# Expert dispatch with one coded product per unit, and routing scans that read PSUM

## The chip, the cores and the metric

The kernel runs on one core of a Trainium2 chip. The metric is the device time in microseconds (us) of one execution; of several executions the median is taken. A core has the engines TensorE (PE in the profile; its weight loads are PEld), VectorE (DVE), ScalarE (ACT), GpSimd (POOL) and SyncE (SP), which run their own instruction streams and wait for each other on semaphores.

## The reference, cut to what matters

One decoder layer: self-attention, cross-attention, then a block of attention and a mixture of experts, on 64 x 256 = 16384 tokens of 256 features. The change touches the part between the router's logits and the experts. Each token picks two of 8 experts; its place in an expert's list is the number of earlier tokens that picked that expert, first choices counted before second choices; an expert takes 4096 tokens.

```python
        logits = x @ wr                                   # x: 16384 tokens x 256, wr: 256 x 8
        top1 = jnp.argmax(probs, axis=-1)
        m1 = jax.nn.one_hot(top1, N_EXPERTS, dtype=x.dtype)
        top2 = jnp.argmax(jnp.where(m1 > 0, -jnp.inf, logits), axis=-1)
        m2 = jax.nn.one_hot(top2, N_EXPERTS, dtype=x.dtype)
        loc1 = jnp.cumsum(m1, axis=0) - 1.0
        loc2 = jnp.cumsum(m2, axis=0) - 1.0 + m1.sum(0, keepdims=True)
        ...
        buf = buf.at[top1, s1].set(x, mode='drop')
        buf = buf.at[top2, s2].set(x, mode='drop')
        h = jax.nn.relu(jnp.einsum('ecd,edf->ecf', buf, w1) + b1[:, None, :])
        y = (jnp.einsum('ecf,efd->ecd', h, w2) + b2[:, None, :]) * (1.0 - MOE_TOKEN_DROPOUT)
        ...
        return g1[:, None] * y1 + g2[:, None] * y2
```

## The kernel before

`program` builds six stages one after the other, with a barrier of all engines between them: `prepare`, three `attention` stages (A, X, F), then `route`, `dispatch` and `experts`. The change is in `route` and `dispatch`.

**Layout.** Token number n*128 + p stands in partition p at tile n, so the logits are a tile of 128 partitions x 128 tiles x 8 experts (`[P, NT, NE]`, 1024 values a partition).

**`route`.** VectorE does nearly all of it in one chain in which each instruction waits for the one before (`chain.step`). It copies the logits to `first`, finds the maximum over experts (`top`), marks it, takes the lowest expert among equals (`rank`), and writes the one-hot choice `one` in float32 and a copy `one_b` in bf16 (L1238, L1239). This happens twice, for the first and the second choice. TensorE multiplies each `one_b` by a matrix of ones below the diagonal (`inside`: earlier tokens of the same tile) and by one of all ones (`whole`: tokens of a tile for each expert), both in PSUM. VectorE then copies `whole` to `hit` (L1250), runs one running sum over tiles for each of 8 experts (L1252), subtracts `hit` again to get the sum of the earlier tiles only (L1254), adds `inside` (L1255), for the second choice also adds the totals of the first (L1258), and picks the token's own expert (L1259, L1260). From that come `scatter`, the place in the list of 8 x 4096 places, split into `high` (which 128-block of the list, 0 to 255) and `low` (which place in the block), and `tail`, the gates.

**`dispatch`.** It inverts that map: for each of the 32768 places, which token stands there. The result is `token` (`[P, 256]`, place low in the partition, block high in the column). There are U = 256 units, one for each tile and choice. For a unit, VectorE writes two tiles of "lines": `by_row` (128 tokens x 128 places: 1 + token's row at the place `low`, else 0, L1335) and `block_of` (128 tokens x 256 blocks: 1 at the block `high`, else 0, L1337). ScalarE scales `by_row` by (1 + tile)/(1 + row) to give `by_tile` (L1352). TensorE multiplies `by_row` by `block_of` into `row_sum` (L1360) and `by_tile` by `block_of` into `tile_sum` (L1362), and both sums run over all 256 units in PSUM. The tiles of lines have R = 4 buffers: VectorE waits on `summed` before it writes one again. At the end four VectorE instructions turn the two sums into `token` (L1340 to L1343). SyncE sends `tail` to the token rows in DRAM at the stage's start (L1311).

**`experts`.** GpSimd gathers token rows by `token` (L1547), TensorE does the two matrix products of each expert (L1466, L1476), ScalarE and VectorE read them out, GpSimd adds the gated rows to the output. Its first instructions come after the barrier behind `dispatch`.

Program order alone sets the order of the work here; the loops over units are written out in full.

Of the kernel before, what the change touches and what calls it, by code (L numbers as in the profile page):

```python
# [5 lines left out]
ALU = mybir.AluOpType  # L6
ACT = mybir.ActivationFunctionType
AX = mybir.AxisListType
P = 128
# [1143 lines left out]
NE = 8  # L1153
# [3 lines left out]
def route(nc, C, D, io):  # L1157
# [3 lines left out]
    with ExitStack() as ctx:  # L1161
# [3 lines left out]
        one = [sb(f"one{i}", [P, NT, NE]) for i in range(2)]  # L1165
        one_b = [sb(f"one_b{i}", [P, NT, NE], BF16) for i in range(2)]
        loc = sb("loc", [P, NT, NE])
        run = [sb(f"run{i}", [P, NT, NE]) for i in range(2)]
# [13 lines left out]
        link, hot, counted, spread_in, exped, b1_in, b1_turned = (  # L1182
            sem(n) for n in ("link", "hot", "counted", "spread_in", "exped", "b1_in", "b1_turned"))
# [7 lines left out]
        def halves(t):  # L1191
            return flat(t).rearrange("p (a w) -> p a w", a=HALF) if HALF > 1 else flat(t)

# [3 lines left out]
        with nc.Block() as block:  # L1197
# [5 lines left out]
            def _(pe):  # L1203
                for i in range(2):
                    pe.wait_ge(hot, i + 1)
                    for a in range(HALF):
                        m = flat(one_b[i])[:, a * W:(a + 1) * W]
# [15 lines left out]
            def _(dve):  # L1223
# [6 lines left out]
                chain.step(v.tensor_copy(flat(first), flat(L)))  # L1230
                down3 = down[:, :].unsqueeze(1).broadcast_to([P, NT, NE])
                for i in range(2):

                    chain.step(v.tensor_reduce(top[i][:, :], first[:, :, :], AX.X, ALU.max))
                    chain.step(v.tensor_tensor(hit[:, :, :], first[:, :, :], wide(top[i]), ALU.is_equal))
# [3 lines left out]
                    v.tensor_copy(flat(one_b[i]), flat(one[i])).then_inc(hot, 1)  # L1239
                    if i == 0:  # L1240
                        chain.step(v.scalar_tensor_tensor(flat(first), flat(one[0]), -3e38, flat(first), ALU.mult, ALU.add))
# [436 lines left out]
```

## Time and profile before

| | us |
|---|---|
| median of 3 executions (5968.39 to 5971.0) | 5969.68 |
| the profiled execution's own time | 5964.57 |
| its span, first to last instruction | 5962.9 |
| `route`, first to last VectorE instruction | 3932.60 to 3984.04 |
| `dispatch`, first to last VectorE instruction | 3985.02 to 4096.76 |
| `experts`, from its first VectorE instruction | 4097.99 |

Times in rows are us from the span's start. A row of the timeline gives start, duration, engine, line, operation and tiles; its duration is that of one instruction from start to end, and neighbours on an engine can overlap, so the step from one start to the next is what a stream costs. Means of one instruction are in ns.

### The profile page before, as it was taken

The page shows a single profiled execution, that of the slowest core. Times are in us where ns is not written, and L with a number is a line of the kernel's source. Part 1 is how long each engine was busy: PE and PEld are TensorE (multiplying, and loading weights), DVE is VectorE, ACT ScalarE, POOL GpSimd, SP SyncE. Part 2 cuts the span into 40 slices and gives each one's busy share as a digit, 9 for nine tenths or more (in the row PEclk, how much of TensorE's full clock was granted, in tenths as well). Part 3 has the DMA queues.
Part 4 walks back from the last instruction along what each step waited for, and adds up shares of the span by engine and source line. Part 5 has one row for each costly group of instructions (what it writes and reads, how often), then busy time and mean ns, then how long its engine had stood idle before and what let it go on. Part 6 is the DMA issues. An engine that isn't in the chain of part 4 may idle for free. (4 is left out here: it accounts for less than half of the span.)

```text
span 5962.9 us, 144169 instructions
## 1 busy us (share of the span) xinstructions
PE 5621.1 (94%) x44441; PEld 4031.8 (68%) x44441; DVE 3721.2 (62%) x10169; ACT 3120.9 (52%) x6803; POOL 2036.6 (34%) x1753
## 2 busy tenths in 40 slices
PE   0999999989999999799999999958999999999998
PEld 0677777667777777577777777734666666666666
DVE  7888888778888887688888888875111111111111
ACT  4788888746666666477777777635121111211111
POOL 0322222233333333244444444401333333333332
PEclk9999999989999999999999999979999999999999
DMA  5777777556666665466766666631222222222221
GB/s 157 178 184 182 182 185 180 148 159 175 174 173 173 174 174 166 120 178 170 182 171 175 177 170 181 168 26 49 39 53 51 33 49 53 32 45 51 38 39 20
DMA packets 625511, 750.10 MB, mean 126 GB/s; under 512 B 131075, under 2 KB 554188, under 8 KB 625328
## 3 DMA queue, kind: packets, MB, share of 16 engines
q1 hardware_dynamic: 568992, 679.62, 43.7%
q0 software_dynamic: 49152, 63.10, 6.6%
q10 hardware_dynamic: 7184, 5.00, 0.3%
q8 instruction: 108, 1.77, 0.1%
q14 instruction: 75, 0.61, 0.0%
HBM read 476.49 MB, written 272.24 MB: 126 GB/s over the span
## 5 line engine op out<-in xcount | busy, mean ns | idle before, releaser
L1488 ACT ACTIVATE exp_hT<-exp_hid,exp_b 128x512 f32<-128x512 f32 x512 | 351.8, 687 | 1487.3 <-PE exp_hid L1466 1372.3
L1476 PE MATMUL exp_res<-exp_w,exp_hT 128*128 128x256 f32 x4096 | 901.2, 381 | 0.8 <-ACT exp_hT L1488 0.8
L1466 PE MATMUL exp_hid<-exp_xT,exp_w 128*128 128x512 f32 x2048 | 891.0, 593 | 0.9 <-DVE exp_xT L1496 0.9
L1476 PEld LDWEIGHTS exp_res<-exp_w,exp_hT 128*128 128x128 f32 x4096 | 773.8, 190 | 112.2 <-ACT exp_hT L1488 1.6
L1566 POOL DMA_INDIRECT out_dram<-exp_gated,exp_token x256 | 406.1, 1586 | 1099.4 <-issue 412.7
L931 DVE TENSOR_REDUCE F_tops<-F_score 128x2 f32<-128x512 f32 x1024 | 684.3, 686 | 59.8 <-PE F_score L685 40.8
L822 ACT ACTIVATE F_probs<-F_scoreT 128x512 f32<-128x512 f32 x1024 | 583.8, 590 | 236.8 <-PE F_scoreT L654 236.8
L1466 PEld LDWEIGHTS exp_hid<-exp_xT,exp_w 128*128 128x128 f32 x2048 | 389.8, 191 | 464.6 <-issue 458.5
L1496 DVE COPY exp_xT<-exp_turn 128x512 f32<-128x512 f32 x128 | 82.6, 686 | 803.2 <-PE exp_turn L1450 803.2
L931 DVE TENSOR_REDUCE A_tops<-A_score 128x3 f32<-128x384 f32 x1024 | 531.6, 554 | 62.3 <-PE A_score L671 54.0
L1532 DVE SCALAR_TENSOR_TENSOR exp_y<-exp_res,exp_b2s 128x512 f32<-128x512 f32 x128 | 88.5, 692 | 735.4 <-PE exp_res L1476 735.4
L822 ACT ACTIVATE A_probs<-A_scoreT 128x384 f32<-128x384 f32 x1024 | 451.0, 488 | 23.1 <-PE A_scoreT L642 14.7
L654 PE MATMUL F_scoreT<-QS,KS 98*128 98x256 bf16 x2048 | 365.4, 275 | 9.7 <-ACT F_probs L822 1.5
L685 PE MATMUL F_score<-KS,QS 96*128 96x256 bf16 x2048 | 362.7, 274 | 8.3 <-DMA KS<-d_k 7.4
L931 DVE TENSOR_REDUCE X_tops<-X_score 128x4 f32<-128x484 f32 x512 | 329.8, 658 | 29.0 <-PE X_score L680 28.9
L822 ACT ACTIVATE X_probs<-X_scoreT 121x512 f32<-121x512 f32 x512 | 295.1, 595 | 78.3 <-PE X_scoreT L650 72.6
L1547 POOL DMA_INDIRECT exp_x<-d_h,exp_token x256 | 269.1, 1051 | 195.6 <-DMA exp_w<-in_L_ffn_w_dram 117.9
L666 PE MATMUL A_score<-causal,ident_b 128*128 128x256 bf16 x1024 | 282.8, 276 | 12.1 <-DMA KS<-d_k 8.3
L638 PE MATMUL A_scoreT<-ident_b,causal 128*128 128x128 bf16 x2048 | 286.1, 221 | 3.2 <-ACT A_probs L822 1.1
L669 PE MATMUL A_score<-KS,QS 96*128 96x256 bf16 x1024 | 281.2, 275 | 0.0
L711 PE MATMUL F_outs<-F_probs,V 128*32 128x256 f32 x4096 | 275.4, 387 | 1.9 <-ACT F_outT L831 1.9
L642 PE MATMUL A_scoreT<-QS,KS 98*128 98x256 bf16 x1024 | 277.2, 271 | 0.0
(330 smaller groups left out, 12099.1 us busy)
## 6 DMA issues: line engine op xcount, KB each, us to landing
QS<-d_q SPq DMA_DIRECT2D x384, 192.0 KB, 3.6
KS<-d_k SPq DMA_DIRECT2D x256, 192.0 KB, 4.0
QS<-d_q SPq DMA_DIRECT2D x384, 128.0 KB, 3.9
KS<-d_k SPq DMA_DIRECT2D x256, 128.0 KB, 4.0
d_q<-A_q_parts SPq DMA_DIRECT2D x64, 384.0 KB, 3.6
d_k<-A_k_parts SPq DMA_DIRECT2D x64, 384.0 KB, 3.9
QS<-d_q SPq DMA_DIRECT2D x384, 64.0 KB, 3.7
d_q<-X_q_parts SPq DMA_DIRECT2D x64, 384.0 KB, 4.0
```

What stands on the lines that cost most here:

```text
L638: mm(s[:, n * P:(n + 1) * P], C["causal"][:, 0:P], ident_b[:, :], start=n == 0, stop=False, skip_group_check=True)
L642: last = mm(s[:, P:384], k[0:98, i, 0:P], q[0:98, i, :], start=False, stop=True, skip_group_check=True)
L654: last = mm(s[:, n * 256:(n + 1) * 256], k[0:98, i, n * P:(n + 1) * P], q[0:98, i, :], start=True, stop=True)
L666: mm(s[:, 0:384].rearrange("p (n k) -> p n k", n=3)[:, 0:3:2, :], ident_b[:, :], C["causal"][:, :].rearrange("p (n k) -> p n k", n=2), sta ...
L669: mm(s[:, P:384], q[0:96, i, P:256], k[0:96, i, :], start=False, stop=False, skip_group_check=True)
L685: last = mm(s[:, n * 256:(n + 1) * 256], q[0:96, i, n * P:(n + 1) * P], k[0:96, i, :], start=True, stop=True)
L822: nc.scalar.activation(probs[m % 2][0:KR, at:at + HB, :].rearrange("p u x -> p (u x)"), scoreT[i % TB][0:KR, 0:HB * TCOL], ACT.Exp)\
L931: nc.vector.tensor_reduce(dst, src, AX.X, ALU.max).then_inc(score_read, 1)
L1466: last = nc.tensor.matmul(h[:, :], w1[k][:, a, f * P:(f + 1) * P], xT[par][:, a, :], start=a == 0, stop=a == 1)
L1476: last = nc.tensor.matmul(res[t][:, s, :], hT[par][:, f, (2 * t + s) * P:(2 * t + s + 1) * P], w2[k][:, f, :], start=f == 0, stop=f == NF - 1)
L1488: nc.scalar.activation(hT[par][:, f, :], hid[f % 2][:, :], ACT.Relu, bias=b1[k][:, f:f + 1])\
L1566: nc.gpsimd.indirect_dma_start(out, bass.IndirectOffsetOnAxis(token[j % (2 * XB)][:, s:s + 1], 0), gated[par][:, s, :], None, bounds_check ...
```

## The change

**In `route`:** `one` is bf16 and is the matrix product's operand, so the casts to `one_b` are gone and TensorE waits on the chain's own semaphore. The first maximum reads the logits in place, so the copy to `first` is gone. The 8 running sums read `whole` straight from PSUM, with a step of 8 values, and write `run` one tile further on (`run` has 129 tiles, its tile 0 is zero or, for the second choice, the first choice's totals, which are also each sum's starting value, given by a pointer). `run[0:128]` is then the sum of the earlier tiles by itself; the copy to `hit`, the subtraction and the addition of totals are gone.

**In `dispatch`:** one product per unit. `by_row` holds 1 + row/128 at the place, `block_of` holds 2^(tile - 64) at the block. Their product is a float whose exponent is the tile and whose upper mantissa bits are the row; the upper 16 bits of the sum, less a constant, are the token's number. `by_tile` and `tile_sum` are gone. Of every five units VectorE writes the lines of four (205 of 256, ring of R = 6) and ScalarE those of the fifth (51 units, ring of RA = 2), in two steps: |column - low| and |column - high| (`gaps`, Abs with a pointer bias), then Relu(value - value * gap), which is the value where the gap is 0 and 0 elsewhere. The gaps of the next ScalarE unit are issued ahead of the second step of this one. TensorE takes the units in their old order.

```diff
--- before.py
+++ after.py
@@ -1162,10 +1162,9 @@
-        one = [sb(f"one{i}", [P, NT, NE]) for i in range(2)]
-        one_b = [sb(f"one_b{i}", [P, NT, NE], BF16) for i in range(2)]
+        one = [sb(f"one{i}", [P, NT, NE], BF16) for i in range(2)]
         loc = sb("loc", [P, NT, NE])
-        run = [sb(f"run{i}", [P, NT, NE]) for i in range(2)]
+        run = [sb(f"run{i}", [P, NT + 1, NE]) for i in range(2)]
...
+        def by_expert(t):
+            return t[:, :, :].rearrange("p a (n e) -> p (a n) e", e=NE)
+
+        def earlier_tiles(i):
+            return run[i][:, 0:NT, :].rearrange("p n e -> p (n e)").rearrange("p (a w) -> p a w", a=HALF)
...
-                    pe.wait_ge(hot, i + 1)
+                    pe.wait_ge(link, CHOSEN[i])
                     for a in range(HALF):
-                        m = flat(one_b[i])[:, a * W:(a + 1) * W]
+                        m = flat(one[i])[:, a * W:(a + 1) * W]
...
-                chain.step(v.tensor_copy(flat(first), flat(L)))
+                v.memset(run[0][:, 0, :], 0.0)
                 down3 = down[:, :].unsqueeze(1).broadcast_to([P, NT, NE])
                 for i in range(2):
-                    chain.step(v.tensor_reduce(top[i][:, :], first[:, :, :], AX.X, ALU.max))
-                    chain.step(v.tensor_tensor(hit[:, :, :], first[:, :, :], wide(top[i]), ALU.is_equal))
+                    scores = (L, first)[i]
+                    chain.step(v.tensor_reduce(top[i][:, :], scores[:, :, :], AX.X, ALU.max))
+                    chain.step(v.tensor_tensor(hit[:, :, :], scores[:, :, :], wide(top[i]), ALU.is_equal))
                     chain.step(v.tensor_tensor(hit[:, :, :], hit[:, :, :], down3, ALU.mult))
                     chain.step(v.tensor_reduce(rank[i][:, :], hit[:, :, :], AX.X, ALU.max))
                     chain.step(v.tensor_tensor(one[i][:, :, :], wide(rank[i]), down3, ALU.is_equal))
-                    v.tensor_copy(flat(one_b[i]), flat(one[i])).then_inc(hot, 1)
+                    assert chain.done == CHOSEN[i]
                     if i == 0:
-                        chain.step(v.scalar_tensor_tensor(flat(first), flat(one[0]), -3e38, flat(first), ALU.mult, ALU.add))
+                        chain.step(v.scalar_tensor_tensor(flat(first), flat(one[0]), -3e38, flat(L), ALU.mult, ALU.add))
...
-                    chain.step(v.tensor_copy(halves(hit), cols(whole[i])))
+                    if i == 1:
+                        chain.step(v.tensor_copy(run[1][:, 0, :], run[0][:, NT, :]))
                     for e in range(NE):
-                        last = v.tensor_tensor_scan(run[i][:, :, e], ones[:, :], hit[:, :, e], 0.0, ALU.mult, ALU.add)
+                        before = 0.0 if i == 0 else run[0][:, NT, e:e + 1]
+                        last = v.tensor_tensor_scan(run[i][:, 1:NT + 1, e], ones[:, :], by_expert(whole[i])[:, :, e], before,
+                                                    ALU.mult, ALU.add)
                     chain.step(last)
-                    chain.step(v.tensor_tensor(flat(loc), flat(run[i]), flat(hit), ALU.subtract))
-                    chain.step(v.tensor_tensor(halves(loc), cols(inside[i]), halves(loc), ALU.add))
-                    if i == 1:
-                        every = run[0][:, NT - 1:NT, :].broadcast_to([P, NT, NE])
-                        chain.step(v.tensor_tensor(loc[:, :, :], loc[:, :, :], every, ALU.add))
+                    chain.step(v.tensor_tensor(halves(loc), cols(inside[i]), earlier_tiles(i), ALU.add))
...
-    R = 4
+    R, RA = 6, 2
     U = 2 * NT
+    SHARE = 5
+    BIAS = 127 - NT // 2
...
+        ON_ACT = [u for u in range(U) if u % SHARE == SHARE - 1]
+        ON_DVE = [u for u in range(U) if u % SHARE != SHARE - 1]
+        powers = power[:, :].bitcast(F32)
...
-                chain = Chain(dve, link, 0, 10, C["passed"])
...
+                chain = Chain(dve, link, 0, 16, C["passed"])
+                chain.step(v.tensor_scalar(place[:, :], C["number"][:, :], 7, None, ALU.logical_shift_right))
+                chain.step(v.tensor_scalar(place[:, :], place[:, :], BIAS, None, ALU.add))
+                chain.step(v.tensor_scalar(power[:, :], place[:, :], 23, None, ALU.logical_shift_left))
+                chain.step(v.tensor_copy(row1[:, :], C["number"][:, 0:1]))
+                chain.step(v.tensor_scalar(row1[:, :], row1[:, :], 1.0 / P, 1.0, ALU.mult, ALU.add))
+                chain.step(v.tensor_scalar(minus[:, :], row1[:, :], -1.0, None, ALU.mult))
+                for i in range(2):
+                    chain.step(v.tensor_scalar(low_minus[i][:, :], C["low"][i][:, :], -1.0, None, ALU.mult))
+                    chain.step(v.tensor_scalar(high_minus[i][:, :], C["high"][i][:, :], -1.0, None, ALU.mult))
                 dve.wait_ge(numbered, 1)
                 chain.step(v.tensor_copy(columns[:, :], column[:, :]))
-                for u in range(U):
-                    n, i, k = u // 2, u % 2, u % R
-                    need(dve, summed, u - R + 1)
+                for d, u in enumerate(ON_DVE):
+                    n, i, k = u // 2, u % 2, d % R
+                    if d >= R:
+                        dve.wait_ge(summed, ON_DVE[d - R] + 1)
                     v.tensor_scalar(by_row[k][:, :], columns[:, 0:P], C["low"][i][:, n:n + 1], row1[:, :],
+                                    ALU.is_equal, ALU.mult)
+                    v.tensor_scalar(block_of[k][:, :], columns[:, :], C["high"][i][:, n:n + 1], powers[:, n:n + 1],
                                     ALU.is_equal, ALU.mult).then_inc(built, 1)
-                    v.tensor_scalar(block_of[k][:, :], columns[:, :], C["high"][i][:, n:n + 1], None, ALU.is_equal)\
-                        .then_inc(built, 1)
                 dve.wait_ge(summed, U)
-                chain.step(v.tensor_copy(rows_of[:, :], row_sum[:, :]))
-                chain.step(v.scalar_tensor_tensor(number[:, :], tile_sum[:, :], float(P), rows_of[:, :], ALU.mult, ALU.add))
+                chain.step(v.tensor_copy(codes[:, :], code_sum[:, :]))
+                chain.step(v.tensor_scalar(upper[:, :], codes[:, :].bitcast(I32), 16, None, ALU.logical_shift_right))
+                chain.step(v.tensor_copy(number[:, :], upper[:, :]))
                 chain.step(v.tensor_scalar(nothing[:, :], number[:, :], 0.0, float(2 ** 20), ALU.is_equal, ALU.mult))
-                v.scalar_tensor_tensor(C["token"][:, :], number[:, :], -float(P + 1), nothing[:, :], ALU.add, ALU.add)\
-                    .then_inc(link, 1)
-                dve.wait_ge(link, 11)
+                chain.step(v.scalar_tensor_tensor(C["token"][:, :], number[:, :], -float(P * BIAS), nothing[:, :], ALU.add,
+                                                  ALU.add))
+                chain.close()
 
             @block.scalar
             def _(act):
-                for u in range(U):
-                    n, k = u // 2, u % R
-                    act.wait_ge(built, 2 * u + 1)
-                    nc.scalar.activation(by_tile[k][:, :], by_row[k][:, :], ACT.Copy, scale=ratio[:, n:n + 1])\
-                        .then_inc(scaled, 1)
+                def gaps(a):
+                    n, i, k = ON_ACT[a] // 2, ON_ACT[a] % 2, a % RA
+                    need(act, shaped, a - RA + 1)
+                    nc.scalar.activation(row_gap[k][:, :], columns[:, 0:P], ACT.Abs, bias=low_minus[i][:, n:n + 1])
+                    nc.scalar.activation(block_gap[k][:, :], columns[:, :], ACT.Abs, bias=high_minus[i][:, n:n + 1])\
+                        .then_inc(spaced, 1)
+
+                act.wait_ge(link, 11)
+                gaps(0)
+                for a, u in enumerate(ON_ACT):
+                    n, k = u // 2, a % RA
+                    if a + 1 < len(ON_ACT):
+                        gaps(a + 1)
+                    act.wait_ge(spaced, a + 1)
+                    if a >= RA:
+                        act.wait_ge(summed, ON_ACT[a - RA] + 1)
+                    nc.scalar.activation(row_a[k][:, :], row_gap[k][:, :], ACT.Relu, bias=row1[:, :], scale=minus[:, :])
+                    nc.scalar.activation(block_a[k][:, :], block_gap[k][:, :], ACT.Relu, bias=powers[:, n:n + 1],
+                                         scale=-(2.0 ** (n - NT // 2))).then_inc(shaped, 1)
 
             @block.tensor
             def _(pe):
                 for u in range(U):
-                    k = u % R
-                    pe.wait_ge(built, 2 * u + 2)
-                    nc.tensor.matmul(row_sum[:, :], by_row[k][:, :], block_of[k][:, :], start=u == 0, stop=u == U - 1)
-                    pe.wait_ge(scaled, u + 1)
-                    nc.tensor.matmul(tile_sum[:, :], by_tile[k][:, :], block_of[k][:, :], start=u == 0, stop=u == U - 1)\
-                        .then_inc(summed, 1)
+                    if u in ON_ACT:
+                        a = ON_ACT.index(u)
+                        pe.wait_ge(shaped, a + 1)
+                        row, blocks = row_a[a % RA], block_a[a % RA]
+                    else:
+                        d = ON_DVE.index(u)
+                        pe.wait_ge(built, d + 1)
+                        row, blocks = by_row[d % R], block_of[d % R]
+                    nc.tensor.matmul(code_sum[:, :], row[:, :], blocks[:, :], start=u == 0, stop=u == U - 1).then_inc(summed, 1)
```

What stands on VectorE between the products and the places of the second choice in `route`, before (`whole` and `inside` are the products in PSUM, `run` the running sums, `one` the choice):

```order
L1250 COPY route_hit<-route_whole 128x1024
L1252 SCALAR_TENSOR_TENSOR route_run<-route_ones,route_hit 128x128 x8
L1254 TENSOR_TENSOR route_loc<-route_run,route_hit 128x1024
L1255 TENSOR_TENSOR route_loc<-route_inside,route_loc 128x1024
L1258 TENSOR_TENSOR route_loc<-route_loc,route_run 128x1024
L1259 TENSOR_TENSOR route_loc<-route_loc,route_one 128x1024
```

and now:

```order
L1258 COPY route_run<-route_run 128x8
L1261 SCALAR_TENSOR_TENSOR route_run<-route_ones,route_run,route_whole 128x128 x8
L1264 TENSOR_TENSOR route_loc<-route_inside,route_run 128x1024
L1265 TENSOR_TENSOR route_loc<-route_loc,route_one 128x1024
```

Two 1024-value instructions around the eight sums (L1250, L1254) and the addition of totals (L1258) are gone, and a copy of 8 values has come (L1258 of the changed kernel). The sums now have a third operand, the starting value. The first choice reads the same without L1258 on either side.

VectorE from the start of `dispatch` to its first unit, before (each later unit repeats the last two rows):

```order
L1324 CAST disp_place<-number 128x128
L1325 TENSOR_SCALAR disp_row<-disp_place 128x1
L1326 TENSOR_SCALAR disp_tile<-disp_place 128x128
L1327 TENSOR_SCALAR disp_tile<-disp_tile 128x128
L1328 RECIPROCAL disp_ratio<-disp_row 128x1
L1329 TENSOR_SCALAR disp_ratio<-disp_tile,disp_ratio 128x128
L1331 CAST disp_columns<-disp_column 128x256
L1335 TENSOR_SCALAR disp_by_row<-disp_columns,low,disp_row 128x128
L1337 TENSOR_SCALAR disp_block_of<-disp_columns,high 128x256
```

and now, behind a first shift (L1339):

```order
L1340 TENSOR_SCALAR disp_place<-disp_place 128x128
L1341 TENSOR_SCALAR disp_power<-disp_place 128x128
L1342 CAST disp_row<-number 128x1
L1343 TENSOR_SCALAR disp_row<-disp_row 128x1
L1344 TENSOR_SCALAR disp_minus<-disp_row 128x1
L1346 TENSOR_SCALAR disp_low_minus<-low 128x128
L1347 TENSOR_SCALAR disp_high_minus<-high 128x128
L1346 TENSOR_SCALAR disp_low_minus<-low 128x128
L1347 TENSOR_SCALAR disp_high_minus<-high 128x128
L1349 CAST disp_columns<-disp_column 128x256
L1354 TENSOR_SCALAR disp_by_row<-disp_columns,low,disp_row 128x128
L1356 TENSOR_SCALAR disp_block_of<-disp_columns,high,disp_power 128x256
```

There are four more instructions ahead of the first unit, and `block_of` reads a second pointer (`power`). The pair of the last two rows stands 205 times instead of 256.

ScalarE from `route` to the end of the unit loop, before:

```order
L1219 ACTIVATE route_other<-route_spread 128x1024
L1220 ACTIVATE route_prob<-route_total 128x128
L1197 UNCONDITIONAL_BRANCH
L1347 UNCONDITIONAL_BRANCH
L1352 ACTIVATE disp_by_tile<-disp_by_row,disp_ratio 128x128 x256
```

and at the start of the loop now (`row_gap` and `block_gap` are the distances, `row_a` and `block_a` the lines):

```order
L1372 ACTIVATE disp_row_gap<-disp_columns,disp_low_minus 128x128
L1373 ACTIVATE disp_block_gap<-disp_columns,disp_high_minus 128x256
L1372 ACTIVATE disp_row_gap<-disp_columns,disp_low_minus 128x128
L1373 ACTIVATE disp_block_gap<-disp_columns,disp_high_minus 128x256
L1385 ACTIVATE disp_row_a<-disp_row_gap,disp_row,disp_minus 128x128
L1386 ACTIVATE disp_block_a<-disp_block_gap,disp_power 128x256
L1372 ACTIVATE disp_row_gap<-disp_columns,disp_low_minus 128x128
L1373 ACTIVATE disp_block_gap<-disp_columns,disp_high_minus 128x256
L1385 ACTIVATE disp_row_a<-disp_row_gap,disp_row,disp_minus 128x128
L1386 ACTIVATE disp_block_a<-disp_block_gap,disp_power 128x256
```

One instruction per unit has become four for every fifth unit, two of 128 and two of 256 columns; a pair of gaps runs one ScalarE unit ahead.

## Rows read from the trace of the kernel before

**Rows 1.** The page: busy us (share of span) xinstructions, and TensorE's granted clock in 40 slices.
```profile
PE 5621.1 (94%) x44441; PEld 4031.8 (68%) x44441; DVE 3721.2 (62%) x10169; ACT 3120.9 (52%) x6803; POOL 2036.6 (34%) x1753
...
PEclk9999999989999999999999999979999999999999
```

**Rows 2.** Busy time by window: PE, PEld, DVE, ACT, POOL; clock; DMA share; GB/s.
```profile
4000.00:4050.00 50.00, 50.00 (x240) 22.83 (x239) 50.00 (x240) 47.88 (x120) 0.00 (x0) 1.00 0.22 2
...
4095.00:4113.00 18.00, 0.05 (x1) 0.00 (x0) 5.42 (x11) 0.00 (x0) 7.61 (x8) 0.60 0.79 264
4113.00:4120.00 7.00, 5.79 (x14) 3.40 (x15) 2.00 (x7) 0.31 (x1) 4.72 (x5) 0.56 0.59 178
```

**Rows 3.** Groups by form, 3984.5 to 4098: busy us, mean ns | idle before, releaser.
```profile
L1352 ACT ACTIVATE disp_by_tile<-disp_by_row,disp_ratio 128x128 bf16<-128x128 bf16 x256 | 102.8, 401 | 40.4 <-DVE disp_by_row L1335 35.8
L1335 DVE TENSOR_SCALAR disp_by_row<-disp_columns,low,disp_row 128x128 bf16<-128x128 bf16 x256 | 76.2, 298 | 0.0
L1360 PE MATMUL disp_row_sum<-disp_block_of,disp_by_row 128*128 128x256 bf16 x256 | 74.1, 289 | 3.9 <-DVE disp_block_of L1337 3.9
...
L1337 DVE TENSOR_SCALAR disp_block_of<-disp_columns,high 128x256 bf16<-128x256 bf16 x256 | 69.0, 269 | 0.0
```

**Rows 4.** Timeline at the start of `dispatch` and of its unit loop.
```profile
3985.02 0.41 DVE L1324 CAST disp_place<-number 128x128 f32<-128x128 int32 x1 [0.97 <-PEq L84]
...
3987.08 0.32 DVE L1335 TENSOR_SCALAR disp_by_row<-disp_columns,low,disp_row 128x128 bf16<-128x128 bf16 x1
3987.31 0.28 DVE L1337 TENSOR_SCALAR disp_block_of<-disp_columns,high 128x256 bf16<-128x256 bf16 x1
...
3987.50 0.31 DVE L1335 TENSOR_SCALAR disp_by_row<-disp_columns,low,disp_row 128x128 bf16<-128x128 bf16 x1
...
3988.07 0.42 PE L1360 MATMUL disp_row_sum<-disp_block_of,disp_by_row 128*128 128x256 bf16 x1
```

**Rows 5.** Timeline at the end of the unit loop.
```profile
4094.20 0.27 DVE L1337 TENSOR_SCALAR disp_block_of<-disp_columns,high 128x256 bf16<-128x256 bf16 x1
...
4095.09 0.43 DVE L1340 COPY disp_rows_of<-disp_row_sum 128x256 f32<-128x256 f32 x1 [0.62 <-PE disp_tile_sum L1362]
4095.55 0.42 DVE L1341 SCALAR_TENSOR_TENSOR disp_number<-disp_tile_sum,disp_rows_of 128x256 f32<-128x256 f32 x1
4096.01 0.29 DVE L1342 TENSOR_SCALAR disp_nothing<-disp_number 128x256 f32<-128x256 f32 x1
```

**Rows 6.** Timeline of `route`, the VectorE instructions that the change touches.
```profile
3933.17 0.63 DVE L1230 COPY route_first<-logits 128x1024 f32<-128x1024 f32 x1
...
3940.12 0.69 DVE L1239 CAST route_one_b<-route_one 128x1024 bf16<-128x1024 f32 x1
3940.73 1.22 DVE L1241 SCALAR_TENSOR_TENSOR route_first<-route_one,route_first 128x1024 f32<-128x1024 f32 x1
...
3954.18 1.22 DVE L1250 COPY route_hit<-route_whole 128x1024 f32<-128x1024 f32 x1
3955.44 2.64 DVE L1252 TENSOR_TENSOR_SCAN route_run<-route_ones,route_hit 128x128 f32<-128x128 f32 x8
3958.11 1.23 DVE L1254 TENSOR_TENSOR route_loc<-route_run,route_hit 128x1024 f32<-128x1024 f32 x1
3959.37 1.23 DVE L1255 TENSOR_TENSOR route_loc<-route_inside,route_loc 128x1024 f32<-128x1024 f32 x1
```

**Rows 7.** Groups by form, VectorE, whole span: same operation with zero, one, two pointers.
```profile
L1018 DVE TENSOR_SCALAR F_xw<-F_xin,F_mean_var,F_rstd 128x256 f32<-128x256 f32 x128 | 51.9, 406 | 0.0
...
L1516 DVE TENSOR_SCALAR exp_b2s<-exp_b 128x256 f32<-128x256 f32 x16 | 4.0, 292 | 0.0
...
L1329 DVE TENSOR_SCALAR disp_ratio<-disp_tile,disp_ratio 128x128 f32<-128x128 f32 x1 | 0.3, 286 | 0.0
...
L1327 DVE TENSOR_SCALAR disp_tile<-disp_tile 128x128 f32<-128x128 f32 x1 | 0.2, 226 | 0.0
```

**Rows 8.** Timeline of ScalarE in `route`: two instructions without pointers.
```profile
3950.33 1.06 ACT L1219 ACTIVATE route_other<-route_spread 128x1024 f32<-128x1024 f32 x1 [20.93 <-DVE route_total L1243]
3951.29 0.29 ACT L1220 ACTIVATE route_prob<-route_total 128x128 f32<-128x128 f32 x1
```

**Rows 9.** DMA issues, 3980 to 4100: KB, us to landing.
```profile
d_h<-tail SPq DMA_DIRECT2D x1, 192.0 KB, 24.7
```

More of the change, by code:

```diff
@@ L1181, in route @@
         whole = [ps(f"whole{i}", [P, HALF, 512]) for i in range(2)]
-        link, hot, counted, spread_in, exped, b1_in, b1_turned = (
-            sem(n) for n in ("link", "hot", "counted", "spread_in", "exped", "b1_in", "b1_turned"))
+        CHOSEN = (5, 11)
+        assert W == 512
+        link, counted, spread_in, exped, b1_in, b1_turned = (
+            sem(n) for n in ("link", "counted", "spread_in", "exped", "b1_in", "b1_turned"))
         def flat(t):
@@ L1299, in dispatch @@
         column, columns = sb("column", [P, HI], I32), sb("columns", [P, HI], BF16)
-        place, row1, tile1, ratio = sb("place", [P, NT]), sb("row1", [P, 1]), sb("tile1", [P, NT]), sb("ratio", [P, NT])
-        by_row, by_tile = [[sb(f"{n}{k}", [P, P], BF16) for k in range(R)] for n in ("by_row", "by_tile")]
-        block_of = [sb(f"block_of{k}", [P, HI], BF16) for k in range(R)]
-        rows_of, number, nothing = sb("rows_of", [P, HI]), sb("number", [P, HI]), sb("nothing", [P, HI])
-        row_sum, tile_sum = ps("row_sum", [P, HI]), ps("tile_sum", [P, HI])
-        numbered, link, built, scaled, summed, tail_out = (
-            sem(n) for n in ("numbered", "link", "built", "scaled", "summed", "tail_out"))
+        place, power = sb("place", [P, NT], I32), sb("power", [P, NT], I32)
+        row1, minus = sb("row1", [P, 1]), sb("minus", [P, 1])
+        low_minus, high_minus = [[sb(f"{n}{i}", [P, NT]) for i in range(2)] for n in ("low_minus", "high_minus")]
+        by_row, block_of = ([sb(f"{n}{k}", [P, m], BF16) for k in range(R)] for n, m in (("by_row", P), ("block_of", HI)))
+        row_gap, block_gap = ([sb(f"{n}{k}", [P, m]) for k in range(RA)] for n, m in (("row_gap", P), ("block_gap", HI)))
+        row_a, block_a = ([sb(f"{n}{k}", [P, m], BF16) for k in range(RA)] for n, m in (("row_a", P), ("block_a", HI)))
+        codes, number, nothing = sb("codes", [P, HI]), sb("number", [P, HI]), sb("nothing", [P, HI])
+        upper = sb("upper", [P, HI], I32)
+        code_sum = ps("code_sum", [P, HI])
+        numbered, link, built, spaced, shaped, summed, tail_out = (
+            sem(n) for n in ("numbered", "link", "built", "spaced", "shaped", "summed", "tail_out"))
+        ON_ACT = [u for u in range(U) if u % SHARE == SHARE - 1]
+        ON_DVE = [u for u in range(U) if u % SHARE != SHARE - 1]
+        powers = power[:, :].bitcast(F32)
         with nc.Block() as block:
@@ L1322, in _ @@
                 v = nc.vector
-                chain = Chain(dve, link, 0, 10, C["passed"])
-                chain.step(v.tensor_copy(place[:, :], C["number"][:, :]))
-                chain.step(v.tensor_scalar(row1[:, :], place[:, 0:1], 1.0, None, ALU.add))
-                chain.step(v.tensor_scalar(tile1[:, :], place[:, :], place[:, 0:1], 1.0 / P, ALU.subtract, ALU.mult))
-                chain.step(v.tensor_scalar(tile1[:, :], tile1[:, :], 1.0, None, ALU.add))
-                chain.step(v.reciprocal(ratio[:, 0:1], row1[:, :]))
@@ L1329, in _ @@
-                chain.step(v.tensor_scalar(ratio[:, :], tile1[:, :], ratio[:, 0:1], None, ALU.mult))
+                chain = Chain(dve, link, 0, 16, C["passed"])
[3 more added lines that the diff above has]
+                chain.step(v.tensor_copy(row1[:, :], C["number"][:, 0:1]))
```

## The prediction

> **What bounds the kernel now.** I read the page's engine line first, then the busy time by window over `dispatch`, the groups by form, the timeline at the loop's two ends, and the timeline of `route`. Over the span TensorE is the busy engine, 94% [rows 1], but that says nothing of the two stages that change. In `route` TensorE has eight products and one transpose; VectorE works through one chain in which each instruction waits for the one before, so each instruction removed gives its whole step back. In the unit loop of `dispatch` four columns are to be compared: VectorE is busy for 50.00 of 50 us, ScalarE for 47.88, TensorE for 50.00 [rows 2]. Three engines look full; one is. A TensorE product is 0.28 to 0.42 us from start to end but they overlap, so its row says little. ScalarE's instruction takes 0.401 [rows 3] against a unit's 0.419, and where ScalarE does not wait it starts the next instruction 0.10 before the last has ended (3950.33 + 1.06 against 3951.29 [rows 8]), so it could go at about 0.30. VectorE has no idle time [rows 3], and it goes at its steady pace from the first unit, when no buffer has yet been used twice: 3987.08, 3987.31, 3987.50, steps of 0.23 and 0.19 [rows 4]. So VectorE sets the pace: (4094.20 - 3987.08 - 0.23) / 255 = 0.419 us a unit [rows 4, 5], 107.3 us for 256. `experts` starts behind a barrier, so what the two stages lose, the span loses.
>
> **`route`, step by step.** Steps are start to start. The copy to `first`: 0.66 (0.63 and 0.03 of hand-over). Two casts: 3940.12 to 3940.73, 0.61 each, 1.22. Two copies of `whole`: 3954.18 to 3955.44, 1.26 each, 2.52. Two subtractions: 3958.11 to 3959.37, 1.26 each, 2.52. One addition of totals, the same form and size: 1.25. Removed: 8.17 [rows 6]. Added: a memset of 8 values, 0.03 (hidden in its neighbours' overlap), and a copy of 8 values, 0.2 (below the 0.226 of a 128-column instruction [rows 7]). Eight of the sixteen running sums get a pointer as starting value. A pointer costs (406 - 292)/2 = 57 ns in the same operation and size with two pointers and with none, and 286 - 226 = 60 ns with one [rows 7]; I take 8 x 0.057 = 0.46, between 0 and 0.9 (twice the row). The sums also read PSUM in place of SBUF. Nothing in the trace shows a running sum from PSUM. The nearest rows are L1255, which reads PSUM, and L1254, which does not: 1.23 both [rows 6]; I take 0. The other end: a plain copy goes from 0.63 (SBUF) to 1.22 (PSUM), so an operand in PSUM can cost a fast rate; the sums take 2.64/8 = 0.33 a step, and if they lost 0.13 each it would be 2.1. A gain is excluded: the same values are read. `one` in bf16 changes nothing for instructions with a second operand that run at 1.22 now. TensorE's products start 0.6 earlier and were long done when read. Sum: -8.17 + 0.03 + 0.2 + 0.46 = -7.5 us.
>
> By the Trainium skill ("VectorE: DVE Perf Modes", section "The TRN2 errata") a VectorE instruction has a fixed part of 58 cycles from SBUF and 120 from PSUM, at 0.96 GHz 65 ns more for each sum; by that rule 16 sums would cost 1.0 us more and the total would be 1.0 us less gain. The trace does not agree for 1024 values, 1.22 to 1.23 us from either memory [rows 6].
>
> **`dispatch`, ahead of the loop.** Now 3985.02 to 3987.08, 2.06 [rows 4]. Then: the first, 0.44; two more shifts of 128 columns at 0.226 + 0.03 = 0.26 [rows 7]; three of one column at about 0.19; four sign changes of 128 columns at 0.26; the cast of `columns`, 0.33: 2.9. Cost +0.8.
>
> **The loop.** `by_row` stays in form. `block_of` gets a second pointer: 0.269 becomes 0.326, the unit 0.419 + 0.057 = 0.476. VectorE has 205 units: 205 x 0.476 = 97.6 against 107.3, -9.7 us. The second pointer is the one price that matters. Below: 0, if it is read beside the first; then 205 x 0.419 = 85.9, -21.4. Above: 0.11, what a pointer costs ScalarE (0.401 with one [rows 3] against 0.29 [rows 8]); then 108.4, +1.1. I take 0.057 because the form with two pointers is there in both element sizes: `by_row` and `block_of` differ by 0.298 - 0.269 = 0.029 with half the columns, which fits 0.057 for the pointer less 0.028 for 128 columns [rows 3, 7].
>
> What is late next? ScalarE: per unit of its own two instructions of 128 and two of 256 columns. From 0.29 for 128 and 1.06 for 1024 a column costs 0.86 ns [rows 8], so 256 take 0.40; a pointer adds 0.11. `row_gap` 0.40, `block_gap` 0.51, `row_a` (two pointers) 0.51, `block_a` 0.51: 1.93 end to end, 1.63 with three overlaps of 0.10, about 1.66 with the wait on its own `shaped`. It has 4 x 0.476 = 1.90 for that. Behind its wait on `summed` (two ScalarE units back, ten units) only its own lines are queued, and TensorE waits for those; VectorE could go ten units before it would notice. At the start ScalarE needs about 2.4 us to its first unit against VectorE's 1.9, which the ring of six covers. TensorE has one product a unit; in the first units, where a product still takes 0.42 from start to end [rows 4], two of them fit into each unit of 0.419, so one fits into 0.476 whatever the clock.
>
> **Behind the loop.** From the last `block_of` to the first read of the sums it is 0.89 now, with ScalarE's copy in between; then 0.33 + 0.28 to 0.42 + 0.06, about 0.15 less. Four closing instructions of 1.67 become five: 0.46 + 3 x 0.33 + 0.42 = 1.87, +0.2 [rows 5]. Together +0.05. SyncE's store of `tail` lands in 24.7 us [rows 9], well inside 98. TensorE's granted clock is 0.60 over the 18 us behind `dispatch` and 0.56 in the next 7 [rows 2], so `experts` starts at the lower level already; at worst 0.50 for 0.56, 0.4 us.
>
> **Sum.** -7.5 + 0.8 - 9.7 + 0.05 = -16.3 us. The profiled execution of 5964.57 becomes 5948.3 us; the median shown is 5.1 above it, so 5969.68 becomes 5953.4.
>
> **Rivals.**
> *The pointer is cheaper than its row* or VectorE's pairs close up further: between -20 and -28 in all, so 5942 to 5950. For it: durations overlap by 0.07 in the loop, and a pointer read could fall there. Against: `by_row` has two and its step, 0.23, is longer than that of `block_of`, 0.19, with twice the columns [rows 4].
> *ScalarE sets the pace.* If its instructions don't overlap (each waits somewhere) a period is 1.93 to 2.07 (four hand-overs of 0.03 more). At 2.0: 51 x 2.0 = 102.0 and 0.9 of lead for the first gaps, 102.9, -4.4 in the loop, -11.1 in all: 5958.6. For it: three of its waits in each unit. Against: all three are on events long past in steady state but the one on `shaped`, and the pairs have no wait inside.
> *`block_of` loses its fast rate* with the second pointer: the slower side. At present it goes at about 0.22 ns a column (the 0.028 above). In float32 the rate is about 0.5 ns ((292 - 226)/128 [rows 7]), in L1254 about 1.04. At that last rate it costs 256 x 0.82 = 0.21 more: 0.686 x 205 = 140.6, +33.3, in all +26.6, 5996.3. At the middle rate the unit is 0.553 and the total -0.6. It turns slower by over 0.2% when a unit takes more than (107.3 + 6.7 + 11.9)/205 = 0.614. Against it: `by_row` has the same form, two pointers and two operations, and 0.298 leaves no room for it.
>
> **Chances.** Forecast as worked out, 0.63, its own range 5950 to 5957. Cheaper pointer 0.17. ScalarE's pace 0.12, a third of it still over the bound. Lost rate 0.06, of which the slowest rate 0.04. Something that gives it back in `experts`, 0.02. The measurement tells about 0.2%, 11.9 us, from no change. Faster 0.63 + 0.17 + 0.04, less 0.03 for noise near the bound: 0.81. Slower 0.05. Same 0.14. The range: 5943, most of the way to the cheap pointer, to 5962, past ScalarE's pace at 2.07 (51 x 2.07 + 0.9, -7.1 in all less the noise).
>
> **What will show it.** `block_of` at about 326 ns and steps of 0.23 and 0.25 in the loop; VectorE without idle time in it and ScalarE idle for 0.2 us or so of each 1.9; the loop in 97 to 98 us; sums in `route` at 0.40 us, eight of them at 0.46. `route` should end 7.5 us earlier. I am wrong if TensorE's waits in the loop are on ScalarE, if `block_of` takes over 0.40, or if the sums from PSUM take over 0.5 each.

## The result and the profile after

| | before | after |
|---|---|---|
| median of 8 executions, us | 5969.49 (5966.25 to 5971.43) | 5952.72 (5949.35 to 5956.41) |
| span of the profiled execution, us | 5962.9 | 5951.0 |

The ratio is 0.9971, its 95% interval 0.996 to 0.9982: the changed kernel is faster by 16.8 us in the medians, by 17 us by the ratio (11 to 24). The forecast was 16.3 us less and 5953.4 us.

The spans differ by 11.9 only. The unchanged stages explain it: `route` begins at 3932.6 us in the profile of before and at 3936.5 in that of after, and in the ten other profiles of this study at 3935.4 to 3939.6. The profile of before was early by 2.8 us or more against all the others, which accounts for over half of the 5 us by which it lay under its median. So stages are compared within each profile. From the first VectorE instruction of `route` to the first of `experts` it is 4097.99 - 3932.60 = 165.4 us before and 4086.20 - 3936.50 = 149.7 after, 15.7 less. From there to the end it is 1864.9 and 1864.8 us: these two profiles show nothing given back, though the same stage takes up to 1866.0 us in other profiles of this study, and 1870.0 in one, so a few tenths would not be seen.

The interval of 11 to 24 us is too wide to test single terms of the forecast; they are tested in the stages below.

Groups by form in `dispatch` of the changed kernel (busy us, mean ns | idle before, releaser), which answer to [rows 3]:

```profile
L1356 DVE TENSOR_SCALAR disp_block_of<-disp_columns,high,disp_power 128x256 bf16<-128x256 bf16 x205 | 67.6, 330 | 0.0
L1354 DVE TENSOR_SCALAR disp_by_row<-disp_columns,low,disp_row 128x128 bf16<-128x128 bf16 x205 | 61.1, 298 | 0.0
L1386 ACT ACTIVATE disp_block_a<-disp_block_gap,disp_power 128x256 bf16<-128x256 f32 x51 | 25.1, 492 | 0.0
L1373 ACT ACTIVATE disp_block_gap<-disp_columns,disp_high_minus 128x256 f32<-128x256 bf16 x51 | 25.1, 492 | 0.0
L1385 ACT ACTIVATE disp_row_a<-disp_row_gap,disp_row,disp_minus 128x128 bf16<-128x128 f32 x51 | 25.0, 491 | 8.9 <-PE disp_code_sum L1400 8.9
```

`block_of` went from 269 to 330 ns, `by_row` stayed at 298, and VectorE still has no idle time. ScalarE's waits are on TensorE (8.9 us), which waits for VectorE's lines: it is ScalarE that has time to spare. The longest waits of the loop show it (who waited for whom: us in total, times, longest us):

```profile
PEld disp_code_sum L1400 <- DVE disp_block_of L1356: 79.7, 204, 5.0
...
PEld disp_code_sum L1400 <- ACT disp_block_a L1386: 0.2, 1, 0.2
```

The timeline at the start of the loop and at its end, for [rows 4, 5]:

```profile
3981.38 0.40 DVE L1339 TENSOR_SCALAR disp_place<-number 128x128 int32<-128x128 int32 x1 [0.98 <-PEq L84]
...
3984.28 0.32 DVE L1354 TENSOR_SCALAR disp_by_row<-disp_columns,low,disp_row 128x128 bf16<-128x128 bf16 x1
3984.51 0.34 DVE L1356 TENSOR_SCALAR disp_block_of<-disp_columns,high,disp_power 128x256 bf16<-128x256 bf16 x1
...
3984.77 0.31 DVE L1354 TENSOR_SCALAR disp_by_row<-disp_columns,low,disp_row 128x128 bf16<-128x128 bf16 x1
...
3986.59 0.40 ACT L1372 ACTIVATE disp_row_gap<-disp_columns,disp_low_minus 128x128 f32<-128x128 bf16 x1
...
3988.20 0.40 ACT L1372 ACTIVATE disp_row_gap<-disp_columns,disp_low_minus 128x128 f32<-128x128 bf16 x1
```

```profile
4082.30 0.33 DVE L1356 TENSOR_SCALAR disp_block_of<-disp_columns,high,disp_power 128x256 bf16<-128x256 bf16 x1
...
4083.11 0.42 DVE L1359 COPY disp_codes<-disp_code_sum 128x256 f32<-128x256 f32 x1 [0.49 <-PE disp_code_sum L1400]
4083.57 0.29 DVE L1360 TENSOR_SCALAR disp_upper<-disp_codes 128x256 int32<-128x256 int32 x1
...
4084.56 0.42 DVE L1363 SCALAR_TENSOR_TENSOR token<-disp_number,disp_nothing 128x256 int32<-128x256 f32 x1
```

The steps are 0.23 and 0.26 where they were 0.23 and 0.19. The loop, first `by_row` to last `block_of`, takes 98.0 us where it took 107.1. A ScalarE unit takes 3988.20 - 3986.59 = 1.61 us while ScalarE is not yet ahead and waits for nothing.

The sums and their neighbours in `route`, for [rows 6]:

```profile
3956.22 2.60 DVE L1261 TENSOR_TENSOR_SCAN route_run<-route_ones,route_whole 128x128 f32<-128x128 f32 x8
3958.85 1.23 DVE L1264 TENSOR_TENSOR route_loc<-route_inside,route_run 128x1024 f32<-128x1024 f32 x1
...
3965.96 0.17 DVE L1258 COPY route_run<-route_run 128x8 f32<-128x8 f32 x1
3966.17 3.08 DVE L1261 TENSOR_TENSOR_SCAN route_run<-route_ones,route_run,route_whole 128x128 f32<-128x128 f32 x8
```

From PSUM eight sums take 2.60 us, from SBUF they took 2.64. With a starting value by pointer they take 3.08, so (3.08 - 2.60)/8 = 0.06 us for each pointer. `route` ends 43.7 us after its first VectorE instruction started, before 51.2 (to the start of its last one).

### The profile page after: what moved, and what is told of

It reads as the page before. It is cut to its first block and busy times, and to the rows that moved or that the text cites. A ratio compares the mean times of both kernels' runs of the same rounds, so it can differ in the third digit from the quotient of the medians.

```text
span 5951.0 us, 143551 instructions
## 1 busy us (share of the span) xinstructions
PE 5601.1 (94%) x44185; PEld 4006.4 (67%) x44185; DVE 3714.2 (62%) x10066; ACT 3103.8 (52%) x6751; POOL 2037.1 (34%) x1753
```

## Experiments

In all of them "the loop" is from the start of the first `by_row` to that of the last `block_of`, and "the two stages" from the first VectorE instruction of `route` to the first of `experts`. Ratios are to the kernel before on the same chip. Where a single execution is given, only its stages are read.

### The two parts apart

Route alone (the kernel before with the new `route`):

> The kernel before with the new route alone. Theory (every step removed from VectorE's chain is given back whole): route is 7.5 us shorter from its first VectorE instruction to the last, dispatch as before at 111.7 us, 5969.5 - 7.5 = 5962.0 us. Rival (part of route's chain waits for something else, so the steps are not given back whole): the trace's route is shorter by less than 7, or dispatch gets longer by what route gained, and the time is 5965 to 5969.

Measured: 5963.43 us, ratio 0.9987 (0.9978 to 0.9996). That is 7.6 us under the kernel before on the same chip. The two stages take 157.8 us, 7.6 less (165.39 - 157.84 = 7.55); the loop is 107.0.

Dispatch alone (the kernel before with the new `dispatch`):

> The kernel before with the new dispatch alone. Theory (the unit loop's pace is VectorE's, 0.479 us for each of its 205 units): the loop takes 98.0 us in place of 107.1, the lines ahead and behind cost 1.0 more, 5969.5 - 8.2 = 5961.3 us. Rival (the two parts need each other, because places arrive earlier or the clock at the start of dispatch differs): the loop is not 98 us here. The gains of this run and of the one with route alone should add up to the 15.7 us that the two stages lost in the profile of the changed kernel.

Measured: 5965.41 us, ratio 0.999 (0.9981 to 0.9999). The two stages take 157.3 us, 8.1 less; the loop is 98.1. The median is 4 us above the expectation, of which 1.6 can be the chip (the kernel before has 5971.07 here, 5969.49 above). The profile's two stages are as expected, but its `experts` took 1870.0 us from the first VectorE instruction, against 1864.8 to 1866.0 in the other profiles, though its code is the same; why it did so in that execution was not found. In the profiles 7.55 + 8.10 = 15.65 is what the two stages lost together (15.69), so the parts add up, and neither hid behind the other. The medians alone, 7.6 and 5.7 less than the kernel before, could not show this: their intervals are 11 us wide.

### The second pointer

```diff
-  v.tensor_scalar(block_of[k][:, :], columns[:, :], C["high"][i][:, n:n + 1], powers[:, n:n + 1],
+  v.tensor_scalar(block_of[k][:, :], columns[:, :], C["high"][i][:, n:n + 1], 2.0 ** (n - NT // 2),
                   ALU.is_equal, ALU.mult)
```

> The changed kernel, with the power of two of block_of given as an immediate: it is the same in every partition, 2^(tile-64). Theory (VectorE sets the pace and the pointer costs 57 to 61 ns an instruction): block_of goes from 330 to about 272 ns, the unit from 0.479 to 0.421, the loop from 98.0 to 86.3 us, 5952.7 - 11.7 = 5941.0 us, and ScalarE, at 1.61 us a unit of its own against VectorE's 1.68 for four, is just short of setting the pace. Rival A (ScalarE or its hand-shake with TensorE sets the pace already; ScalarE waits 8.9 us on summed): the loop stays at 97 to 98 us. Rival B (any second operation costs it, pointer or not): block_of stays at 330 ns and the loop at 98.

Measured: 5941.54 us, ratio 0.9949 (0.9935 to 0.9963). It is the fastest kernel of this study (it comes once more below, as the immediate alone). By tile (min/median/max ns, first and last start):

```profile
L1354 DVE TENSOR_SCALAR disp_by_row<-disp_columns,low,disp_row x205: 302/323/355, 3986.1 to 4071.5; 128x128 bf16<-128x128 bf16 x103
L1356 DVE TENSOR_SCALAR disp_block_of<-disp_columns,high x205: 274/295/328, 3986.3 to 4071.7; 128x256 bf16<-128x256 bf16 x103
```

From the timeline's starts the loop is 4071.74 - 3986.05 = 85.7 us, 12.3 less, so the pointer cost 12.3/205 = 0.060 us a unit. Rivals A and B both fall. The duration did not come as expected, 295 ns and not 272, and `by_row`, which nobody touched, went from 297 to 323; yet the unit fell to 0.419. The price is in the steps, not in the durations.

### Who sets the pace

No unit on ScalarE:

```diff
-        ON_ACT = [u for u in range(U) if u % SHARE == SHARE - 1]
-        ON_DVE = [u for u in range(U) if u % SHARE != SHARE - 1]
+        ON_ACT = []
+        ON_DVE = list(range(U))
```

> The changed kernel, but VectorE writes the lines of all 256 units and ScalarE none. Theory (VectorE's pace): 256 x 0.479 = 122.7 us in the loop, 24.7 longer than with the share, so the coded product without the share would be 15.6 us slower in the loop than the old loop of 107.1; time about 5977. Rival (TensorE at the lower clock, or the ring, sets the pace): the loop stays near 98 us.

Measured (one execution, 5980.64 us): the first `by_row` and the last `block_of` are

```profile
3987.31 0.32 DVE L1354 TENSOR_SCALAR disp_by_row<-disp_columns,low,disp_row 128x128 bf16<-128x128 bf16 x1
...
4109.85 0.33 DVE L1356 TENSOR_SCALAR disp_block_of<-disp_columns,high,disp_power 128x256 bf16<-128x256 bf16 x1
```

The loop takes 122.5 us, so the rival falls. The coded product without the share is slower than the kernel before, because all it does for VectorE is to add a pointer.

Every fourth unit on ScalarE:

```diff
-    SHARE = 5
+    SHARE = 4
```

> The changed kernel with every fourth unit on ScalarE instead of every fifth. Theory (the slower of the two engines sets the pace: VectorE 3 x 0.479 = 1.44 us, ScalarE 1.61 us a period of four units): ScalarE becomes the bound, 64 x 1.61 = 103 us in the loop, 5 longer than with every fifth, with VectorE waiting some 10 us in all. Rival (ScalarE's share has slack left, because its 1.61 holds waits that go away): the loop follows VectorE, 192 x 0.479 = 92 us.

Measured (one execution): the loop is 101.1 us. Its longest waits (who waited for whom: us in total, times, longest us):

```profile
PEld disp_code_sum L1400 <- ACT disp_block_a L1386: 65.9, 63, 1.1
...
PE disp_code_sum L1400 <- ACT disp_block_a L1386: 36.3, 63, 0.6
```

TensorE's products wait for ScalarE in 63 periods, where in the changed kernel its weight loads wait for VectorE. ScalarE sets the pace, 63 x 1.61 = 101.4. The rival falls. At its own pace VectorE would take 192 x 0.479 = 92.0 us, so it loses 9.1 in the loop; its idle column shows 4.5 of that, since in an undisturbed stream the next instruction starts before the last has ended. The expected 103 counts all 64 ScalarE units. The last unit of all is now ScalarE's, and the first read of the sum comes 2.69 us after the last `block_of` where it came after 0.81: 101.1 + 1.9 = 103.0.

Two of nine on ScalarE (one line as above, `u % 9 in (4, 8)`):

> The changed kernel with two of nine units on ScalarE. Theory: VectorE 7 x 0.479 = 3.35 us, ScalarE 2 x 1.61 = 3.22 us a period of nine, so VectorE still sets the pace: 200 x 0.479 = 95.4 us in the loop, 2.6 shorter. Rival (with less slack the hand-shakes show): 97 to 99 us.

Measured (one execution): the loop is 95.7 us, as the theory has it to 0.3.

The same with the immediate:

> The power as an immediate and two of nine units on ScalarE. Theory (the slower engine sets the pace): VectorE 7 x 0.421 = 2.95, ScalarE 2 x 1.61 = 3.22, so ScalarE sets it: 28.4 x 3.22 = 91.6 us, longer than the 86.3 of the immediate with every fifth unit. Rival (only VectorE counts): 200 x 0.421 = 84.2 us.

Measured (one execution): the loop is 4073.75 - 3983.25 = 90.5 us, 4.8 longer than with every fifth unit. VectorE waits for TensorE (4.7 us in 23 waits) and TensorE's products for ScalarE (25.5 us in 54 waits). It is 56 ScalarE units x 1.61 = 90.2; the expectation's 91.6 counted 57.

### TensorE and its clock

```diff
+  nc.tensor.matmul(spare[:, 0:HI], row[:, :], blocks[:, :], start=u == 0, stop=u == U - 1)
   nc.tensor.matmul(code_sum[:, 0:HI], row[:, :], blocks[:, :], start=u == 0, stop=u == U - 1).then_inc(summed, 1)
```

(`spare` is a new PSUM tile; it and `code_sum` are declared 512 wide, of which 256 are used.)

> The changed kernel with a second product of each unit's lines into a PSUM tile that nothing reads, so TensorE has its old 512 products. Theory (TensorE is no bound, the removed product by itself gave nothing, ScalarE's freed time did): the loop stays at 98 us, and the granted clock in it rises from 0.50 towards the 1.00 of before; experts takes the same 1864.8 us with either clock. Rival A (TensorE at the lower clock does set the pace): two products need 0.43 us at the lower clock and the loop gets 2 us or more longer, unless the clock rises. Rival B (the lower clock at the end of dispatch costs experts something): experts gets shorter by 0.4 us or more.

Measured (one execution): the loop is 98.1 us. Busy time by window (PE, PEld, DVE, ACT, POOL; granted clock; DMA share; GB/s) in the changed kernel, the loop, the 18 us behind it and the next 7:

```profile
4000.00:4050.00 50.00, 43.43 (x132) 11.57 (x130) 50.00 (x210) 44.18 (x105) 0.00 (x0) 0.50 0.08 1
...
4083.00:4101.00 18.00, 0.08 (x1) 0.00 (x0) 5.58 (x12) 0.00 (x0) 7.40 (x8) 0.50 0.74 260
4101.00:4108.00 7.00, 5.63 (x13) 3.27 (x14) 2.04 (x7) 0.10 (x1) 4.93 (x5) 0.54 0.61 183
```

and with the second product:

```profile
4000.00:4050.00 50.00, 43.06 (x261) 16.91 (x262) 50.00 (x209) 44.25 (x107) 0.00 (x0) 1.00 0.32 3
...
4104.00:4111.00 7.00, 6.12 (x15) 3.43 (x16) 2.02 (x7) 0.69 (x1) 4.30 (x5) 0.61 0.52 160
```

With one product a unit the granted clock stays at 0.50 of full, 1.2 GHz, through the whole loop; with two it is at 1.00, 2.4 GHz, as before the change. The loop takes the same time. Two products a unit at 1.00 keep up with 98.1/256 = 0.383 us a unit, less than the 0.419 of before, so TensorE was no bound there and the removed product in itself gave nothing. Against rival A this run alone is weak, since the clock rose with the second product. The run with the immediate settles it: with one product a unit and the clock at 0.50 its loop took 85.7 us, so TensorE at the lower clock is no bound at 98. Its window:

```profile
4000.00:4050.00 50.00, 48.00 (x151) 13.22 (x150) 50.00 (x240) 48.99 (x125) 0.00 (x0) 0.50 0.33 2
```

`experts` took 1864.9 us behind this loop and 1864.8 behind the one at half clock. No cost of the lower clock is seen, but against rival B this is weak: 0.4 us is less than the 1.2 by which most profiles of this study differ in that stage.

### GpSimd takes a share

Beginning with the immediate, of twelve units one goes to GpSimd, two to ScalarE and nine to VectorE:

```diff
+                for d, u in enumerate(ON_POOL):
...
+                    nc.gpsimd.tensor_scalar(row_p[k][:, :], columns[:, 0:P], C["low"][i][:, n:n + 1], row1[:, :],
+                                            ALU.is_equal, ALU.mult)
+                    nc.gpsimd.tensor_scalar(block_p[k][:, :], columns[:, :], C["high"][i][:, n:n + 1], 2.0 ** (n - NT // 2),
+                                            ALU.is_equal, ALU.mult).then_inc(pooled, 1)
```

> The kernel with the immediate (loop 85.6 us), and of every twelve units nine on VectorE, two on ScalarE and one on GpSimd, which is idle in the loop. No row shows GpSimd writing such lines; its nearest, a product of two 128x512 float32 tiles, takes 1.26 us. Theory (GpSimd's unit takes under the period of 9 x 0.419 = 3.77 us and disturbs nobody): the loop follows VectorE, 192 x 0.419 = 80.4 us, 5.2 shorter than with the immediate alone, about 5936 us. Rival A (VectorE's instructions get longer while GpSimd works on the same memory): its unit goes above 0.446 on average and the loop is 85.6 or longer. Rival B (GpSimd's unit takes longer than 3.77 us): GpSimd sets the pace and TensorE waits for it.

> The kernel with the immediate once more, on the same chip as the GpSimd share, so that the two can be compared. Theory: loop 85.6 us and 5941 to 5942 us as measured before; a ratio of 0.995 to the kernel before. If the ratio is nearer to 0.998 the first measurement was a matter of the chip.

Measured on one chip: the GpSimd share 5942.4 us, ratio 0.9948 (0.9934 to 0.9961); the immediate alone 5938.07 us, ratio 0.994 (0.9926 to 0.9954). The share's timeline over one of its periods:

```profile
4040.49 0.90 POOL L1342 TENSOR_SCALAR disp_row_p<-disp_columns,low,disp_row 128x128 bf16<-128x128 bf16 x1 [1.91 <-PE disp_code_sum L1416]
...
4040.74 0.38 DVE L1368 TENSOR_SCALAR disp_block_of<-disp_columns,high 128x256 bf16<-128x256 bf16 x1
...
4041.04 0.40 DVE L1366 TENSOR_SCALAR disp_by_row<-disp_columns,low,disp_row 128x128 bf16<-128x128 bf16 x1
...
4041.38 1.29 POOL L1344 TENSOR_SCALAR disp_block_p<-disp_columns,high 128x256 bf16<-128x256 bf16 x1
...
4041.46 0.46 DVE L1366 TENSOR_SCALAR disp_by_row<-disp_columns,low,disp_row 128x128 bf16<-128x128 bf16 x1
...
4043.30 0.31 DVE L1366 TENSOR_SCALAR disp_by_row<-disp_columns,low,disp_row 128x128 bf16<-128x128 bf16 x1
...
4044.58 0.89 POOL L1342 TENSOR_SCALAR disp_row_p<-disp_columns,low,disp_row 128x128 bf16<-128x128 bf16 x1 [1.92 <-PE disp_code_sum L1416]
```

The period is 4044.58 - 4040.49 = 4.09 us for nine VectorE units in place of 3.77. GpSimd needs 2.2 us for its unit and then waits 1.9, so rival B falls; but while it works, VectorE's instructions last up to 0.46 and its steps widen. Over the whole loop, the mean step of `by_row` is 0.272 us where it lies wholly inside a GpSimd instruction (86 of them) and 0.224 where it lies outside (88); that of `block_of` is 0.217 (79) against 0.195 (102). So a unit costs 0.489 us while GpSimd works and 0.419 while it does not, and VectorE has no idle time in either. The loop is 87.2 us against 85.8 for the immediate on the same chip: 193 VectorE units at 0.452 against 205 at 0.419. Rival A holds. The two stages differ by 1.4 us as the loops do, 138.8 against 137.4; the medians differ by 4.3, and where the other 2.9 come from was not found. Whether the two engines contend for a memory port, or for `columns`, which both read, no run here tells. The immediate alone was expected at 5941 to 5942 us and a ratio of 0.995; its loop is as expected, its median 3 us lower.

## Why the prediction was right

Point by point, forecast against the profiles:

| step | forecast, us | measured, us |
|---|---|---|
| `route` | -7.5 | -7.5 (51.2 to 43.7) |
| ahead of the loop | +0.8 | +0.8 (2.06 to 2.90) |
| the loop | -9.7 | -9.1 (107.1 to 98.0) |
| last lines to first read of the sum | -0.15 | -0.1 (0.89 to 0.81) |
| closing instructions | +0.2 | +0.2 (1.67 to 1.87) |
| `experts` | 0 to +0.4 | -0.1 (1864.9 to 1864.8) |
| sum | -16.3 | -15.7 in the two stages, -16.8 in the medians |

That the medians agree with the forecast to 0.5 us is partly luck: their interval is 13 us wide. The agreement of the single terms in the stages is not.

*`route`.* The removed instructions, priced by their own steps, gave back the sum that the chain of waits lets one expect. The added copy, forecast 0.2, steps by 0.21 (3965.96 to 3966.17), and the eight pointers, forecast 0.46, took 3.08 - 2.60 = 0.48.

*The bound of the loop.* That VectorE sets the pace was read off two rows, no idle time and the steady pace from the first unit on. Taking away ScalarE's share made the loop longer by 24.5 us, taking away a pointer shorter by 12.3, a second product did nothing. This is shown.

*The pointer.* Forecast 0.057 from instructions of other shapes, measured 0.060 in the loop (with and without it) and 0.06 in the sums (by steps; their durations are 459 against 400 ns). The 0.003 is the 0.6 us by which the loop missed. The rival in which it is hidden falls, and so does the one in which `block_of` loses its fast rate.

*ScalarE.* Forecast 1.66 us a unit of its own against VectorE's 1.90 for four, measured 1.61 against 1.92. It does set the pace as soon as its share is a quarter, and with the immediate two of nine are too many. The rival was real, only one step away from this share. Its sum for the slow end slips: 51 x 2.07 + 0.9 = 106.5 us is -7.5 in all, not -7.1, which moves neither the forecast nor a chance.

*PSUM.* The sums last 400 ns from PSUM, 403 from SBUF, and eight of them take 2.60 against 2.64 us. Forecast at 0 from two rows of another instruction, this held. The rule of the Trainium skill, page "VectorE: DVE Perf Modes", section "The TRN2 errata", by which PSUM adds 62 cycles, is not seen in this instruction; by an estimate from that figure the gain would have been 1.0 us smaller.

*What was not foreseen.* The better change lay inside the price that I named as the one that matters: the power of two is the same in all partitions, so the pointer was never needed. The change's two edits in the loop work against each other. The coded product costs VectorE 0.06 a unit, and it pays only because it frees ScalarE for a fifth of the units: 107.1 to 122.5 us by the first, then to 98.0 by the second. Whether ScalarE could have taken a smaller share beside the two old products was not tried.

## What to carry to other kernels

Where three engines look busy, find the one that keeps its steady pace from the first turn of the ring, and price an edit in its steps; an operation taken from another engine is worth only the work that this engine can then take over. Before a value goes in by a pointer, ask whether it differs between partitions at all: here the pointer cost 0.06 us for each of 205 instructions. Balance a share by the measured period of each engine (1.61 us against 4 x 0.48), and measure again when either price changes.

## What the runs showed that I had not expected

- An instruction's duration is no price. The same `by_row` lasts 298 ns in the profile of before, 328 in the run with the new `route` alone and 323 with the immediate, at the same 0.419 us a unit.

```profile
L1341 DVE TENSOR_SCALAR disp_by_row<-disp_columns,low,disp_row 128x128 bf16<-128x128 bf16 x256 | 84.0, 328 | 0.0
L1343 DVE TENSOR_SCALAR disp_block_of<-disp_columns,high 128x256 bf16<-128x256 bf16 x256 | 76.6, 299 | 0.0
```

  (Groups by form of the run with the new `route` alone; its loop of 107.0 us compares with 107.1 for the 298 and 269 ns of [rows 3].) The new `route` by itself is not the reason, as the changed kernel has it too and shows 298. What sets the duration was not found.
- GpSimd writes 128x256 lines in 1.27 us where VectorE's step is 0.19, and slows VectorE by 8% over its period (0.452 against 0.419 us a unit).
- TensorE's granted clock stayed at 0.50 through 98 us with one product a unit, and was 1.00 with two. The loop took the same time with either, and no difference was seen in `experts`.
